# A Swin attention block with its MLP on one Trainium2 core: MLP data turned in 32x32 blocks by VectorE, maxima split on token rows

## The reference

```python
y = layernorm(x, g1, b1); y = roll(y, (-2, -2)); xw = windows(y)          # (8*16, 128, 32)
q, k, v = split(xw @ qkv_w + qkv_b); q = q * SCALE
attn = softmax(q @ k.T + bias + mask)                                     # (8*16, 4, 128, 128)
o = roll(unwindow(attn @ v @ proj_w + proj_b), (2, 2))
x = x + o
z = layernorm(x, g2, b2)
return x + gelu(z @ fc1_w + fc1_b) @ fc2_w + fc2_b
```

## Time and profile before

| | |
|---|---|
| time, median of 3 runs | 245.58 us (244.77 to 246.78) |
| time of the profiled execution | 244.59 us |
| its span (first to last instruction) | 242.8 us, so 1.8 us lie around it |
| busy: PE, DVE, ACT, POOL | 213.5, 166.4, 148.4, 110.2 us |
| granted TensorE clock, mean | 0.968 |
| loop steps p = 0 to 63 | 35 to 213 us of the span |
| MLP stage | about 213 to 240 us |

### The profile page before, as it was taken

The page is one execution under the profiler, slowest core; times in us unless marked ns, Lnnn a source line. Parts: engine busy times, 40 slices in busy tenths (PEclk is TensorE's granted clock), DMA queues, the critical chain, the costliest instruction groups (busy, mean ns, idle before and its releaser), DMA issues.

```text
span 242.8 us, 8095 instructions
## 1 busy us (share of the span) xinstructions
PE 213.5 (88%) x3344; PEld 121.5 (50%) x3344; DVE 166.4 (69%) x268; ACT 148.4 (61%) x219; POOL 110.2 (45%) x77
## 2 busy tenths in 40 slices
PE   0176489899999999999999999999999999988983
PEld 0143233465565556655665665566556655533331
DVE  5856546575886879687868785777676666557553
ACT  8362235666774777576667766766545665597660
POOL 6636982164309841891388068520801430403500
PEclk9999657999999999999999999999999999999998
DMA  6828635545504632263264035304610000001222
GB/s 196 224 67 255 183 126 180 176 136 178 155 7 155 196 99 74 84 188 109 90 185 125 10 123 165 113 9 156 199 49 1 4 5 5 3 0 43 96 107 102
DMA packets 25495, 26.57 MB, mean 109 GB/s; under 512 B 3744, under 2 KB 22944, under 8 KB 25344
## 3 DMA queue, kind: packets, MB, share of 16 engines
q1 hardware_dynamic: 24356, 25.08, 32.9%
q10 hardware_dynamic: 1104, 0.99, 1.5%
HBM read 17.01 MB, written 8.78 MB: 106 GB/s over the span
## 4 chain that ended last, share of the span: by engine, by line
issue 35%; PE 34%; POOL 19%; DVE 4%; ACT 3%; DMA 2%; ACTq 1%; POOLq 0%; DVEq 0%
PE pav L856 5%; POOL rstd L341 5%; PE ps L823 5%; POOL parts L355 4%; POOL xc L333 4%; PE ps L836 3%; PE ps L791 3%; PE ps L873 2%; POOL yn L348 2%; PE pch L935 2%; POOL X L361 2%; PE pav L887 2%; PE pch L923 2%; ACT prob L653 2%; PE ps L809 2%
## 5 line engine op out<-in xcount | busy, mean ns | idle before, releaser
L454 DVE TENSOR_REDUCE negm<-ps 128x8 f32<-128x1024 f32 x64 | 78.0, 1221 | 29.2 <-PE ps L809 28.9
L653 ACT ACTIVATE prob<-ps 128x1024 f32<-128x1024 f32 x64 | 65.4, 1022 | 28.8 <-PE ps L836 28.8
L341 POOL TENSOR_TENSOR rstd<-var,neghalf 128x16 f32<-128x16 f32 x16 | 47.0, 2936 | 73.5 <-DVE var L425 73.4
L823 PE MATMUL ps<-rel_j,id_b 96*32 96x512 bf16 x512 | 40.1, 387 | 2.3 <-ACT prob L653 2.3
L856 PE MATMUL pav<-prob,va 128*32 128x128 f32 x1024 | 41.2, 279 | 0.0
L856 PEld LDWEIGHTS pav<-prob,va 128*32 128x32 f32 x1024 | 24.1, 109 | 13.1 <-issue 6.3
L809 PE MATMUL ps<-k_rows,q_rows 64*128 64x128 bf16 x512 | 25.9, 223 | 4.1 <-DMA k_rows<-slots 4.0
L791 PE MATMUL ps<-rel_i,ident_b 64*64 64x512 bf16 x256 | 27.2, 415 | 0.2 <-DVE negm L454 0.2
L836 PE MATMUL ps<-q_rows,k_rows 64*128 64x128 bf16 x512 | 25.6, 220 | 0.1
L355 POOL TENSOR_TENSOR parts<-rest,parts 128x512 bf16<-128x512 f32 x16 | 18.5, 1159 | 15.2 <-ACT parts L637 15.2
L648 ACT ACTIVATE m_hi<-pq 16x128 bf16<-16x128 f32 x32 | 8.4, 264 | 25.7 <-PE pq L779 25.7
(11 more groups left out here) (108 smaller groups left out, 308.3 us busy)
## 6 DMA issues: line engine op xcount, KB each, us to landing
slots<-parts SPq DMA_DIRECT2D x24, 256.0 KB, 2.5
q_rows<-slots SPq DMA_DIRECT2D x42, 128.0 KB
k_rows<-slots SPq DMA_DIRECT2D x42, 128.0 KB
X<-x_tok SPq DMA_DIRECT2D x8, 256.0 KB, 3.7
y_tok<-res SPq DMA_DIRECT2D x7, 256.0 KB, 2.0
q_rows<-slots SPq DMA_DIRECT2D x12, 64.0 KB, 2.4
k_rows<-slots ACTq DMA_DIRECT2D x12, 64.0 KB, 2.5
q_rows<-m_hi SPq DMA_DIRECT2D x32, 4.0 KB
```

The lines of the kernel that those rows point to most:

```text
L341: pool.tensor_tensor(rstd[:, i, :], var[:, i, :], neghalf[:], ALU.pow).then_inc(rstd_done[i], 1)
L454: dve.tensor_reduce(dst, first_home(j)[:].rearrange("p (a u n) -> p a u n", u=2, n=TOK), AX.X, ALU.max, negate=True).then_inc(max_done, 1)
L653: act.activation(prob[:, j % NPROB, :], ps2[:], ACT.Exp).then_inc(exp_done, 1)
L823: pe.matmul(ps2[32 * c:32 * (c + 1), 512 * e:512 * (e + 1)], id3_b[0:96, :], rel_j[0:96, c, e].unsqueeze(2).to_broadcast([96, 2, 2, TOK]), ...
```

## The change

Six things are changed.

- The second norm's result yn (tokens on partitions) is turned by one `dve.transpose` of 128 x 512 on VectorE in blocks of 32x32 (`channels_second`, at step 6 of image m+2) in place of four TensorE transposes and a copy. An image's window has 32 channels, and so the blocks hold what `fc1` needs, with 32 tokens of each window in a quadrant.
- The result of `fc2` is turned back in the same way (`mlp_tokens`, from PSUM to m_tok), in place of `mlp_out` and `transpose_out`. The bias of fc2 is added to the image beforehand by GpSimd (`add_mlp_bias`, 128 x 512, once per image). The results of `fc2` alternate between two banks.
- The maxima are split into bf16 high and middle parts while still on token rows, by two VectorE instructions (`split_max`, after `row_max` of each odd step); one bf16 product with 32 columns against ident_b turns both (`transpose_max`), one ScalarE copy takes them out (`max_rows`), and one DMA sends them.
- `middle_max` on even steps and its second DMA are gone.
- Norm and split work is placed in other steps: on VectorE first means at step 0 (was 1), second remainder at 3 (was 4); on ScalarE second high part at 2 (was 3), middle parts after the exponential of steps 1 and 3 (were ahead of that of 2 and 4), second square at 5 (was 6); on GpSimd first centre at 1 (was 2), second centre at 4 ahead of the low part (was 5, behind it), first power and scale at 5 (were 4 and 6).
- In the last stage `fc1(0)` stands behind the scores of pair 62 (was ahead of them), and TensorE's list is `fc1(m)`, `fc2(m-1)` in turn with no transposes.

```diff
@@ maxima
-            def middle_max(k):
-                dve.wait_ge(mhi_done, k + 1)
-                after(dve, d_m[k % 2], 32 * (k // 2))
-                dve.tensor_tensor(m_mid[:, k % 2, :], Q1[0:16, 0:TOK], m_hi[:, k % 2, :],
-                                  ALU.subtract).then_inc(mmid_done, 1)
+            def split_max(k):
+                by_head = negm[:, k % 2].rearrange("p (e a) -> p e a", e=2)
+                split = m_parts[:, k % 2].rearrange("p (e f a) -> p f e a", e=2, f=2)
+                dve.wait_ge(max_done, 2 * k + 2)
+                after(dve, mT_done, k - 1)
+                dve.tensor_copy(split[:, HIGH], by_head).then_inc(mhi_done, 1)
                 dve.wait_ge(mhi_done, k + 1)
+                dve.tensor_tensor(split[:, MID], by_head, split[:, HIGH], ALU.subtract).then_inc(mmid_done, 1)
...
-                if p < 0:
+                if p < PAIRS - LEAD:
                     row_max(p + LEAD)
-                if p % 2 == 0 and 0 <= (p + 2) // 2 < GROUPS:
-                    middle_max((p + 2) // 2)
-                if 0 <= p < PAIRS - LEAD:
-                    row_max(p + LEAD)
+                    if p % 2 == 1:
+                        split_max((p + LEAD) // 2)
...
             def transpose_max(k):
-                pe.wait_ge(max_done, 2 * k + 2)
+                pe.wait_ge(mmid_done, k + 1)
                 if k:
-                    pe.wait_ge(mmid_done, k)
+                    pe.wait_ge(mrow_done, k)
...
-                pe.transpose(Q1[0:16, 0:TOK], negm[:, k % 2, :], P("ident")).then_inc(mT_done, 1)
+                pe.matmul(Q1[0:32, 0:TOK], m_parts[:, k % 2, :], ident_b[:], start=True, stop=True).then_inc(mT_done, 1)
...
+            def max_rows(k):
                 act.wait_ge(mT_done, k + 1)
-                after(act, d_m[k % 2], 32 * (k // 2))
-                act.activation(m_hi[:, k % 2, :], Q1[0:16, 0:TOK], ACT.Copy).then_inc(mhi_done, 1)
+                after(act, d_m[k % 2], 16 * (k // 2))
+                act.activation(m_rows[:, k % 2, :], Q1[0:32, 0:TOK], ACT.Copy).then_inc(mrow_done, 1)
@@ MLP
-            def mlp_out(m, lo=0, hi=512):
+            def mlp_tokens(m, lo=0, hi=512):
                 dve.wait_ge(fc2_done, m + 1 + lo // 256)
-                after(dve, mlp_done, m)
-                dve.tensor_scalar(mT2[:, lo:hi], mlp_home(m, lo)[:, lo:hi], P("fc2b"), None, ALU.add).then_inc(mT2_done, 1)
+                after(dve, res_done, m)
+                dve.transpose(m_tok[:, lo:hi], mlp_home(m, lo)[:, lo:hi]).then_inc(mtok_done, 1)
...
-            def copy_yT2(m, src):
+            def channels_second(m):
                 i, seq = second_norm(m)
-                dve.wait_ge(yTp_done[i], seq + 1)
-                dve.tensor_copy(yT2[:, m, :], src).then_inc(yT2_done, 1)
+                dve.wait_ge(yn_done[i], seq + 1)
+                dve.transpose(yT2[:, m, :], yn[:, i, :]).then_inc(yT2_done, 1)
...
+            def add_mlp_bias(m):
+                pool.wait_ge(xc_done[1], m + 2)
+                pool.tensor_tensor(per_window(img(m)), per_window(img(m)),
+                                   P("fc2b").unsqueeze(1).to_broadcast([128, WPI, C]), ALU.add).then_inc(xmb_done, 1)
...
-            fc2(1)
-            transpose_out(0)
-            fc1(3)
-            transpose_out(1)
...
+            for m in range(3, B):
+                fc1(m)
+                fc2(m - 1)
+            fc2(B - 1)
```

More of the change, by code:

```diff
@@ L346, in scale @@
                 pool.wait_ge(xc_done[i], seq + 1)
-                after(pool, yTp_done[i], seq)
+                if i == 1 and seq:
+                    after(pool, yT2_done, seq - 1)
+                else:
+                    after(pool, yTp_done[i], seq)
                 pool.tensor_tensor(per_window(yn[:, i, :]), per_window(xc[:, i, :]),
@@ L381, in _ @@
                     scale(second_norm(b - 2))
-                if s == 2 and b < B:
-                    add_proj_bias(b)
-                if s == 2 and b + 3 < B:
+                if s == 1 and 0 <= b - 2 < B - 2:
+                    add_mlp_bias(b - 2)
+                if s == 1 and b + 3 < B:
                     center(first_norm(b + 3), b + 3)
@@ L404, in _ @@
             scale(second_norm(B - 1))
+            add_mlp_bias(B - 1)
         @block.vector
@@ L436, in scale @@
                 i, seq = t
+                if i == 1 and seq:
+                    after(dve, yT2_done, seq - 1)
                 dve.wait_ge(rstd_done[i], seq + 1)
@@ L598, in _ @@
             for m in range(2, B - 1):
-                mlp_out(m)
+                mlp_tokens(m)
                 add_residual(m)
-                if m == B - 4:
-                    copy_yT2(B - 1, ps2[:, 0:512])
+                if m == B - 5:
+                    channels_second(B - 1)
             for half in range(2):
-                mlp_out(B - 1, 256 * half, 256 * (half + 1))
-            for half in range(2):
+                mlp_tokens(B - 1, 256 * half, 256 * (half + 1))
                 add_residual(B - 1, 256 * half, 256 * (half + 1))
@@ L889, in fc2 @@
                     mm.then_inc(fc2_done, 1)
-            def transpose_out(m, first=0, last=NG):
-                pe.wait_ge(mT2_done, m + 1 + first // 2)
-                if m == 0:
-                    pe.wait_ge(x2_done, OCTETS)
-                after(pe, res_done, m)
-                for g in range(first, last):
-                    mm = pe.transpose(out_home(128 * first)[:, 128 * g:128 * (g + 1)], mT2[:, 128 * g:128 * (g + 1)], P("ident"))
-                mm.then_inc(mlp_done, 1)
             pe.wait_ge(w_ready, 1)
@@ L986, in _ @@
                     scores_s1(p + LEAD)
+                if p == PAIRS - 2:
+                    fc1(0)
             project_out(OCTETS - 2)
             weighted_values(PAIRS - 2)
-            pe.wait_ge(exp_done, PAIRS)
-            transpose_second(B - 2, ps2)
             weighted_values(PAIRS - 1)
@@ L994, in _ @@
             fc1(1)
+            channels_first(OCTETS - 1)
             fc2(0)
-            channels_first(OCTETS - 1)
+            project_out(OCTETS - 1)
             fc1(2)
-            project_out(OCTETS - 1)
             fc2(1)
-            transpose_out(0)
-            fc1(3)
-            transpose_out(1)
-            fc2(2)
-            fc1(4)
-            transpose_out(2)
-            fc2(3)
-            fc1(5)
-            transpose_out(3)
-            fc2(4)
-            fc1(6)
-            transpose_out(4)
-            pe.wait_ge(gelu_done, 2 * (B - 2))
-            transpose_second(B - 1, ps2)
-            fc2(5)
-            fc1(7)
-            transpose_out(5)
-            fc2(6)
-            fc2(7)
-            transpose_out(6)
-            for half in range(2):
-                transpose_out(B - 1, 2 * half, 2 * half + 2)
+            for m in range(3, B):
+                fc1(m)
+                fc2(m - 1)
+            fc2(B - 1)
 def _to_tokens(x):
```

122 lines of the change are left out of this document (52 added, 70 removed).

## The result

The changed kernel takes 247.44 us (median of 20 runs, 244.72 to 250.25) against 244.81 us for the kernel before on the same chip (median of 20, 244.05 to 246.78): ratio 1.008, 95% interval 1.005 to 1.010. It is slower by 0.8%, where 240.7 and "faster" had been forecast. The time itself is that of rival B, 247.3. The profiled execution took 245.3 us, with a span of 243.5; before it was 242.8. Of the changed kernel's 20 times seven lie between 244.7 and 246.1, eleven between 247.0 and 248.3, and two near 250, which the ratio leaves out; the profiled execution is of the first group, so 2.1 us of the median are in no trace and stay unexplained.

The account below looks back on a forecast made before the run. TensorE, busy 213.5 of 242.8 us, was taken to bound the kernel. From 244.59 us, +0.2 for the loop and -4.3 for the MLP stage and end gave 240.5, plus 0.2 for the median 240.7; range 238.0 to 248.0.

Parts of the forecast that it names:

- rival B: GpSimd's low part starts first and holds the split's subtraction: 0.95 us at seven places, 6.6 in all, 247.3 us; chance 0.27.
- VectorE against GpSimd: The open point: whether GpSimd's low part (L355) holds up the split's subtraction on VectorE, 0.95 us at each of seven places.
- case A: The forecast itself: the split's subtraction mostly gets through beside GpSimd's low part; 240.7 us, chance 0.50.
- The start: Start of the loop: the split comes into the chain of the first maxima, +0.4 us.
- The maxima without clashes: Even steps of the loop: TensorE's new wait for the split against cheaper turning of the maxima, together +2.1 us.
- The second norm's transposes, -1.8: Loop: six sets of four TensorE transposes go, -0.30 us each, -1.8 in all.
- the norms' places, -1.5: Step 7: ScalarE's wait for GpSimd's centred tile goes, -0.59 us once and -0.30 for images 2 to 4.
- VectorE's transpose, +1.35: Step 6: a 0.69 us transpose delays the row maximum; TensorE waits about 0.27 us at step 7, images 2 to 6.
- rival C: VectorE's transpose costs 1.4 us: 3.5 more in the loop, 0.8 in the MLP stage, 245.0 us; chance 0.10.
- add_mlp_bias, nothing: GpSimd's addition of fc2's bias, 8 times 1.27 us, ahead of the first centre, costs nothing in itself.
- The MLP stage, -4.3: Last stage: 2.38 us per image in place of 2.65 and a shorter end, 2.45 for 4.1; together -4.3 us.
- Rival D: The MLP stage stays at 2.65 us per image and only the end is shortened, 243.4 us; chance 0.13.

Follow-up runs that it names:

- e4: The changed kernel with the edits of e1 and e2 together; 237.83 us, ratio 0.970 to the kernel before.
- e3: The changed kernel with the maxima carried as before the change (f32 transposes, two DMAs); 235.96 us, ratio 0.962 to the kernel before.
- e2: The changed kernel with the split's first instruction, a cast, written as a reduction over an axis of length one; 243.95 us, ratio 0.997.
- e1: The changed kernel with GpSimd's low part, from image 2 on, waiting for the split of the step before; 239.24 us, ratio 0.975.
- e5: e4 with the product that turns the maxima moved behind bias_s1 in TensorE's list; 234.45 us, ratio 0.958 to the kernel before.
- e6: e3 with the norms and the split of the projections back at their old steps, VectorE's transpose kept; 239.82 us, ratio 0.980.
- e8: e5 with GpSimd's addition of fc2's bias to image 6 moved behind its last scale; 235.68 us, ratio 0.963 to the kernel before.

## Why the prediction was wrong

**The step that failed is "VectorE against GpSimd"**, as case A took it: "the subtraction mostly gets through (it is queued within 0.1 us of L355, and GpSimd has to start up)". It never got through. GpSimd had started 0.07 to 0.09 us earlier, and seven places cost 6.15 us in the loop. The prediction had the place, the number of places and nearly the price; what it had against it was that L417 and L355 within 0.1 us of each other had not been seen to cost in the steps. That was a misreading. Where the two stood so close, at 161.97 and 162.08 in the trace of before, VectorE was the first. And with GpSimd first the same trace has the clash in its steps, in step 1 of images 2, 3 and 4:

```profile
129.74 1.27 POOL L361 TENSOR_TENSOR X<-X,pb_full 128x512 f32<-128x512 f32 x1
...
130.31 0.74 DVE L417 TENSOR_SCALAR mean<-ssum 128x16 f32<-128x16 f32 x1
...
131.62 1.21 DVE L454 TENSOR_REDUCE negm<-ps 128x8 f32<-128x1024 f32 x1
```

L417 takes 0.74 to 0.76 us in place of 0.17. The row maximum starts 1.97 us after the step's L823, where it is 1.56 in image 5, and the step behind takes 2.82 to 2.97 us in these images and 2.62 in images 1 and 5. The order in the earlier trace rows put the subtraction 0.08 after L355, and those two starts should have decided. Rival B deserved the larger chance, and A the smaller.

**The start** was a second clash of the same kind that no rival had. The +0.4 was the split by itself; e4, free of the fill but with one subtraction still held, has 0.75 more than e3. The cast beside the fill adds 1.3 (e2) to 1.5 (e4, both against after), and 1.1 to 1.2 of it are still there at pair 8. Together +1.4 against before, since the rest of the change took 0.8 off the start (e3 against before).

**The maxima without clashes** were forecast at +2.1, of which the terms for images 1 to 7 make +1.7. e4 against e3 has +1.94 there, and the signs and sizes hold step by step: +0.16 at steps 2 and 6 for +0.14, +0.11 at step 4 for +0.06, -0.17 at step 0 for -0.14. This term was right. The wait after the row maximum is as long as reckoned: in e1 it ends at 153.85 and the product starts at 154.33, 0.48. The product takes 0.16 from its start to the next instruction where I took 0.07, inside the bounds named, and that makes the waits a little dearer. e5 shows that the wait could be had for nothing.

**The second norm's transposes, -1.8, and the norms' places, -1.5.** With the -0.3 of the loop's end the three terms made -3.6, against -4.3 measured (e3 against before, pairs 8 to 63). Singly they were wrong: -0.6 (e6 against before) and -3.7 (e3 against e6). I had costed the removal at step 6 without asking what it uncovers at step 7. And "in all 64 steps TensorE's list is nearly without gaps" was not so at step 2 of images 2 to 4, where the new places took 0.8 away (e3 against before). The forecast had put nothing there, neither for moving the means nor for the second DMA, which was late in image 3 of before (the weight load of L836 waits 0.4 us for it).

**VectorE's transpose, +1.35.** Its duration was right, 0.70 us against 0.69, and rival C fell with it. The wait of TensorE at step 7 did not come: in step 6 the row maximum started 0.07 after its data were ready, and step 7 takes 2.98 us, under the 3.06 named as the most it could be. The 0.1 us to spare that I had estimated was too little. In e5, whose step 6 is 0.21 shorter, 0.1 us of the wait is there (step 7 at 3.08).

**add_mlp_bias, nothing:** right as placed. e8 shows that it was not free of place: moved 17 us later it costs 1.4.

**The MLP stage, -4.3:** measured -4.37 from pair 63 to the end of the last sum. The cycle is 2.43 against 2.38, the end 2.43 against 2.45; the two terms named for the end, 0.6 and four pieces of 0.42, make only 2.28, and the rest stood there without its working. Rival D is out. The granted clock did not fall with TensorE's waits there. Part 2 of the page, 40 slices, in tenths:

```profile
PEclk9999657999999999999999999999999999999997
```

Only slices 5 to 7 (24 to 43 us), around the beginning of the loop, and the last one, with the end of the outputs, are under 0.9.

The forecast's span, which had no clash in it, would have been 240.5 - 1.8 = 238.7. e4 has 235.9, 2.8 less: 1.35 is the wait that did not come and 0.7 lies ahead of pair 8; the rest is what the new places gave beyond their 1.5, less what the maxima cost beyond their 1.7.

## What to carry to other kernels

Before an edit puts a small VectorE instruction on the path, look at which GpSimd operations run beside it in the trace: with two SBUF inputs or as a plain copy, an instruction of 0.17 us cost as much as was left of theirs (the power apart). Look for it in the old trace first, at every place where GpSimd starts ahead: one instruction far over its median is the sign. A wait that lets the small one go first, or a form of it that is not held, takes the cost away (here 6.3 and 1.3 us of span). Compare two kernels over a stretch in which clock and DMA waits are the same. When a removed piece stood just ahead of a wait, count it as gained only as far as the wait does not grow.

## What the runs showed of the hardware

- A reduction over an axis of length one works as a cast from f32 to bf16 at the copy's price (0.17 us for 128x16) and was not held by either GpSimd operation beside it, while the copy was held 1.77 us by a fill.
- A fill of 128x2064 on GpSimd held a cast and not a subtraction with two SBUF inputs; the low part (128x512, which reads SBUF) held both (0.78 and 0.85 us at the start, 1.11 in the loop), the instruction that started first keeping its normal time.
- GpSimd's power (128x16, two SBUF inputs, 2.9 us) held neither cast nor subtraction, in eleven places each.
- GpSimd's own operations were longer in the MLP stage, beside VectorE's: the power 3.29 us (2.91 in its last turn in the loop), the scale 1.35 (1.07 in the mean of all). That VectorE's work is the cause was not tested.
- VectorE turns 128x512 of f32 in 32x32 blocks in 0.70 us from SBUF and 0.72 from PSUM, 128x256 in 0.45: the price of a copy of that size.
